# Carry, mean, variance, refinement steps and row maximum kept in spare columns of VectorE's own PSUM bank

## The reference, cut to what matters

```python
def _layernorm(x, axis=-1, eps=1e-05):
    m = jnp.mean(x, axis=axis, keepdims=True)
    v = jnp.var(x, axis=axis, keepdims=True)
    return (x - m) / jnp.sqrt(v + eps)

# attention, for each time step, batch row b and head h (16 heads of d = 16)
hebbian = jnp.einsum('bhi,bhj->bhij', v_t, k_t)
state = retention[None] * state + Gamma[None] * hebbian
y_t = jnp.einsum('bhij,bhj->bhi', W_static[None] + state, q_t)

# linear layer: each token is scaled by its own absolute maximum
amax = jnp.clip(jnp.max(jnp.abs(x), axis=-1, keepdims=True), EPS, None)
scale = amax / QMAX
x_q = jnp.clip(jnp.round(x / scale), -128, 127)

h = tok(x)                       # base + 0.1 * sum over domains of corrections
h = h + attn(_layernorm(h))
h = h + ffn(_layernorm(h))
```

## Time and profile before

| what | value |
|---|---|
| median of 3 runs | 365.59 us (363.73 to 366.17) |
| span of the profiled execution | 360.0 us |
| median above that span | 5.6 us |
| instructions | 4155 |
| DVE busy | 302.0 us (84%) |
| PE busy | 274.5 us (76%) |
| POOL busy | 207.5 us (58%) |
| ACT busy | 183.8 us (51%) |

### The profile page before, as it was taken

One profiled execution on the slowest core, in us unless ns is written; L12 is line 12 of the kernel. 1 busy time (PEld: TensorE's weight loads), 2 busy tenths in 40 slices (PEclk: granted clock), 3 DMA queues, 4 the chain that ended last, 5 costly groups with the idle time before them and its releaser, 6 DMA issues. The chain is left out here.

```text
span 360.0 us, 4155 instructions
## 1 busy us (share of the span) xinstructions
PE 274.5 (76%) x1214; PEld 141.5 (39%) x1214; DVE 302.0 (84%) x443; ACT 183.8 (51%) x336; POOL 207.5 (58%) x175
## 2 busy tenths in 40 slices
PE   5786899965979777965998498559978546747792
PEld 4674225531322353632333366223324213205581
DVE  0144098999999999999999999999999999999262
ACT  3236593455654704775768037576763168610152
POOL 5777676447873913747768317547876158970010
PEclk9899995996898799896999989887996956859899
DMA  6711200000010000000111000000210000001001
GB/s 168 251 46 49 75 7 2 3 0 0 13 50 26 0 3 1 0 0 29 36 50 33 4 1 0 0 31 0 74 44 3 0 0 0 0 15 46 0 2 58
DMA packets 10502, 10.07 MB, mean 28 GB/s; under 512 B 3344, under 2 KB 8944, under 8 KB 10480
## 3 DMA queue, kind: packets, MB, share of 16 engines
q1 hardware_dynamic: 9200, 7.70, 7.1%
q0 software_dynamic: 1280, 2.11, 2.1%
HBM read 4.95 MB, written 2.10 MB: 20 GB/s over the span
## 5 line engine op out<-in xcount | busy, mean ns | idle before, releaser
L380 POOL TENSOR_TENSOR uu<-vg,kk 128x512 f32<-128x512 f32 x128 | 160.1, 1275 | 99.7 <-ACT vg L566 93.7
L566 ACT ACTIVATE vg<-vr_ps,gam_sb 128x512 f32<-128x512 f32 x128 | 83.1, 687 | 20.3 <-PE vr_ps L882 12.6
L690 DVE TENSOR_TENSOR_SCAN zz<-r_ps,uu 128x512 f32<-128x512 f32 x64 | 77.2, 1214 | 10.3 <-POOL uu L380 10.3
L690 DVE TENSOR_TENSOR_SCAN zz<-r_ps,carry,uu 128x512 f32<-128x512 f32 x64 | 79.1, 1273 | 0.0
L711 DVE TENSOR_TENSOR zz<-zz,q_ps 128x1024 f32<-128x1024 f32 x64 | 76.4, 1196 | 0.0
L882 PE MATMUL vr_ps<-v_rows,selv 96*128 96x512 bf16 x100 | 40.5, 441 | 18.3 <-ACT vg L566 18.1
L896 PE MATMUL y_ps<-zz,sely 128*32 128x512 f32 x256 | 41.0, 717 | 15.2 <-DVE zz L711 15.2
L882 PEld LDWEIGHTS vr_ps<-v_rows,selv 96*128 96x128 bf16 x100 | 9.7, 102 | 55.8 <-ACT vg L566 38.9
L352 POOL TENSOR_TENSOR tok<-tok,bf 128x1024 f32<-128x1024 f32 x4 | 9.4, 2357 | 30.9 <-ACT tmp_b L482 29.3
L423 ACT ACTIVATE tok<-scr 128x512 f32<-128x512 f32 x16 | 9.5, 591 | 24.4 <-PE scr L812 17.5
L760 PE MATMUL scr<-wexp,emb_t 128*128 128x256 f32 x64 | 20.6, 479 | 1.0 <-ACT emb_t L415 1.0
(11 more groups left out here) (95 smaller groups left out, 413.3 us busy)
## 6 DMA issues: line engine op xcount, KB each, us to landing
v_rows<-v_part SPq DMA_DIRECT2D x84, 32.0 KB, 1.9
out_h<-tok SPq DMA_DIRECT2D x8, 256.0 KB, 2.2
wexp<-in_w_exp SPq DMA_DIRECT2D x1, 256.0 KB, 2.8
tok<-in_table,ids_sb POOLq DMA_INDIRECT x16, 2.8
wproj<-in_w_proj SPq DMA_DIRECT2D x1, 256.0 KB, 5.0
wv<-in_w_v SPq DMA_DIRECT2D x1, 256.0 KB, 4.8
wk<-in_w_k SPq DMA_DIRECT2D x1, 256.0 KB, 4.9
wq<-in_w_q SPq DMA_DIRECT2D x1, 256.0 KB, 5.3
```

What stands on the lines that cost most here:

```text
L380: pool.tensor_tensor(uu[:, slot % NU, :], vg[:, slot % NVG, :], kk[:, c % 2, hg, :], ALU.mult).then_inc(s_u, 1)
L566: act.activation(vg[:, slot % NVG, :], vr_ps[:, slot % NVR, :], ACT.Copy, scale=gam_sb[:, n:n + 1]).then_inc(s_vg, 1)
L690: dve.tensor_tensor_scan(zz[:, g % NZ, :], r_ps[:, n:n + 1].to_broadcast([P, T]), uu[:, g % NU, :], start, ALU.mult, ALU.add).then_inc(s_s ...
```

## The change

`carry`, `mv`, `am` and two of the three columns of `nr` lose their SBUF tiles and become views of `r_ps`: carry in columns 32 to 63, mean and variance in 64 to 79, the refinement's products in 80 to 95, the row maximum in 104 to 107. The reciprocal of the root stays in SBUF as `root`. The Newton step is written in another order: before, half the square of the root, times `ve`; now variance plus epsilon times the root, and that times minus one half times the root. So `ve` is read by ACT alone. The order of the instructions on every engine, their number and all semaphores are as before.

```diff
-        carry = sb("carry", [P, UNITS])
-        mv = sb("mv", [P, 2, TT, 2])
-        nr = sb("nr", [P, 2, 3, TT])
+        root = sb("root", [P, 2, TT])
-        am = sb("am", [P, TT])
...
         r_ps = ps("r_ps", [P, T])
+        carry = r_ps[:, UNITS:2 * UNITS]
+        mv = r_ps[:, 64:80].rearrange("p (n t s) -> p n t s", n=2, s=2)
+        nr = r_ps[:, 80:96].rearrange("p (n i t) -> p n i t", n=2, i=2)
+        am = r_ps[:, 104:108]
...
-                    r0, half_sq, fix = (nr[:, n, i, two] for i in range(3))
+                    r0, prod, fix = root[:, n, two], nr[:, n, 0, two], nr[:, n, 1, two]
                     link(dve.reciprocal(r0, sd[:, n, two]))
-                    link(dve.scalar_tensor_tensor(half_sq, r0, -0.5, r0, ALU.mult, ALU.mult))
-                    link(dve.tensor_tensor(fix, half_sq, ve[:, n, two], ALU.mult))
+                    link(dve.scalar_tensor_tensor(prod, mv[:, n, two, 1], LNEPS, r0, ALU.add, ALU.mult))
+                    link(dve.scalar_tensor_tensor(fix, prod, -0.5, r0, ALU.mult, ALU.mult))
                     link(dve.scalar_tensor_tensor(rstd[:, n, two], fix, 1.5, r0, ALU.add, ALU.mult))
```

## The result

The changed kernel takes 335.21 us (median, 334.41 to 339.93), the kernel before 364.71 us beside it (363.73 to 366.17). The ratio is 0.9185 with a 95% interval of 0.9138 to 0.9233: faster, by 29.5 us. The profiled execution has a span of 333.8 us and took 335.75 us; the span before was 360.0 us.

The account below looks back on a forecast made before the run. VectorE was taken to bound the kernel from first scan to last product. Gains of 9.7 + 12.8 + 7.3 = 29.8 us, less 1.3 and 0.5 off the path, gave 365.6 - 28.0 = 337.6, said as 338 us; range 334 to 352.

Parts of the forecast that it names:

- The bound and the cause: From first scan to last product VectorE is busy 283.64 of 289 us; its small all-SBUF operations wait for POOL.
- The terms of the gain: Waits removed on VectorE: carry copies 9.7 us, refinement steps 12.8, xs and ve 7.3, together 29.8 us.
- What is off the path: Of the 29.8 us, 1.3 near the first scans and masks and 0.5 at xs gain nothing, leaving 28.0.
- The stall at 54.28: A 0.73 us VectorE stall whose removal gains nothing, since VectorE idles 1.24 us before a mask at 62.06 anyway.
- What lies around the span: Median of timed runs 365.59 us, 5.6 above the profile's 360.0 us span; the change touches nothing outside the span.
- The price of PSUM operands: Scans and short VectorE operations newly using PSUM cost 0 extra; bounds 13.2 us dearer to 3.8 us cheaper.
- the nmr step: Two SBUF inputs yet a mean of 161 ns over 16, so the shared-port rule isn't the whole story.
- One-source operations that go on waiting: Rival: copies into PSUM and tensor_scalars out of it still wait for POOL; 17.0 us stay, 355 us; chance 0.08.
- Dearer PSUM: Rival: PSUM reads cost 59 ns each, giving 343 us on 88 short operations, 351 on all 224; chance 0.12.
- the slower case: Rival: each of 64 scans waits for the PSUM bank to drain; at 0.55 us each, 373 us; chance 0.03.
- Feeders: Rival: POOL, ScalarE and PE take back a third of the gain once a lead falls below zero; 347 us; chance 0.10.
- The change does nothing: Rival: the stall comes from small operations in a row, not from where operands lie; 366 us; chance 0.03.

Follow-up runs that it names:

- e5_poolwrite: The kernel before, with POOL's 128 products replaced by a memset of uu to a constant, so POOL writes without reading; one execution, 337.93 us.
- e4_reduce: The kernel before, carry still in SBUF but written by a tensor_reduce over one element instead of a tensor_copy; 357.83 us, ratio 0.9859.
- e8_onecol: The kernel before, with the carry copied by two tensor_copy instructions of one column each, SBUF to SBUF; 358.97 us, ratio 0.987.
- e6_order: The kernel before, with the refinement in the new order and all buffers in SBUF; 363.91 us, ratio 1.0012.
- e7_wlo_pool: The changed kernel, with the subtraction for the lowest part of the quantized weights moved from VectorE to POOL; 332.39 us, ratio 0.9151 to the kernel before.
- e3_am: The kernel before, with only the row maximum moved into the PSUM bank of r_ps; 358.35 us, ratio 0.9788.
- e1_carry: The kernel before, with only the carry tile moved into the PSUM bank of r_ps; 353.80 us, ratio 0.9735.
- e2_steps: The changed kernel, but with carry and the row maximum kept in SBUF as before; 345.39 us, ratio 0.9529 to the kernel before.
- the last three experiments: The changed kernel again, then with the weights' subtraction on POOL, then also with extra idle-time PE matmuls; 363.84, 361.92, 362.93 us, the kernel before 393.94.

## Why the prediction was right, by its steps

**The bound and the cause: right.** VectorE's busy time was the path, and its small operations waited for POOL. That they waited for POOL is shown by e5_poolwrite, where POOL's reading is gone and with it the wait of the steps, and by the ends: from the first scan on, every one over 0.25 us ends 0.01 to 0.03 us behind a POOL instruction. e4_reduce and e8_onecol (same data, same place, no wait) show that it takes a certain kind of access, and e6_order that the new order of the steps does nothing by itself.

**The terms of the gain: right.** Copies 32 x (442 - 149) = 9.4 us (predicted 9.7); steps 16 x (516 - 168 + 478 - 168 + 289 - 159) = 12.6 (12.8); xs and ve 8 x (902 - 160) + 16 x (260 - 159) = 7.6 (7.3). The sum is 29.6 for 29.8, and busy time fell by 29.2. The prediction didn't count the subtraction of e7_wlo_pool, which waits before and after.

**What is off the path: right in the stretch, wrong in the tail.** The stretch was to lose 28.0 less the tail's 1.5, 26.5 us; it lost 26.1. The stall at 54.28 was indeed taken back at 62 us, by a wait that grew by 0.74. The 1.5 us in the tail were gained too: from the first tok of the tail to the end there are 17.8 us where there were 19.3, and so it is in e3_am, where only the maximum moved. But from the last product to that tok there were 7.8 us where there had been 6.5, with PE's sum of y and first output matmuls at the lower level; at the higher one it is 4.9 (e7_wlo_pool, with 22.8 us of tail). So the tail as a whole lost only 0.2 us, and the span 26.2 for the predicted 28.0. The prediction had no term for PE's clock behind the last product, which differs between executions of one kernel.

**What lies around the span: the mis-sized term.** The prediction put 5.6 us around the span, the difference between the median and one profiled execution. The changed kernel's profiled execution took 335.75 us with a span of 333.8: 1.95 us around it. The other 3.6 us were the distance between a short execution and the median. Beside e5 to e8, 16 of 17 executions of the kernel before ranged over 360.95 to 364.93 us. The median therefore fell by more (29.5) than the two profiled spans did (26.2), and the forecast of 338 was 2.8 us too high. That 28.0 lies between the two is in part luck, since PE's clock in the tail alone moves a profiled span by up to 3 us. It may also be why a usual execution of the kernel before is longer than the profiled one; that wasn't settled.

**The price of PSUM operands: right, close to zero.** Scans that take their start value from PSUM stay at 1273 ns in the mean of the 64, those without one at 1214 (VectorE's timeline of the changed kernel: a scan without a carry, then one that starts from it):

```profile
108.10 1.21 DVE L691 TENSOR_TENSOR_SCAN zz<-r_ps,uu 128x512 f32<-128x512 f32 x1
...
110.34 1.28 DVE L691 TENSOR_TENSOR_SCAN zz<-r_ps,uu 128x512 f32<-128x512 f32 x1
```

Writing PSUM costs 7 to 9 ns more (the copy 149 against the 140 of a free one, steps 168 against 161), reading it 10 less for the two tensor_scalar operations (ve 159 against 169) and 2 less for nmr and rstd. The Trainium skill's 62 extra cycles for PSUM as the source ("VectorE: DVE Perf Modes", section "The TRN2 errata — SBUF-src ops pay a fixed extra latency per instruction") don't show in this case: ve, xs and nmr read PSUM at 159 to 160 ns.

**A reading that was wrong.** The prediction took the nmr step, two SBUF inputs and 161 ns, as a sign that the rule on shared ports isn't the whole story. It was a matter of when: nmr stands behind three steps that wait for POOL's running product, and in none of its 16 executions was a product running when it began. Before the change, nmr starts at 87.10 us, behind the rstd step that ends at 87.07, and the six products of the earlier trace rows end at 87.05. With that, the rule of the Trainium skill ("SBUF — State Buffer", section "Who interferes with whom") agrees with what was measured, down to the two sorts of wait in e5_poolwrite: two SBUF inputs contend with POOL's reading alone, two-port modes with its writing too. What it doesn't tell is why xs waited there for several memsets in a row (last section).

**The rivals.** One-source operations that go on waiting: refuted, copy and xs are short. Dearer PSUM, and the slower case with it: refuted. Feeders: POOL's narrowest lead after 62 us fell from 1.2 to 0.8 us, and never to zero. The change does nothing: refuted. A rival that the prediction didn't have, that the stall shifts to the next operation, may be true in part when only some of the operations are freed: 2.7 of 5.9 us in e3_am and 2.1 of 10 in e4_reduce, but 0.2 of 9.4 in e1_carry, and in e2_steps the rest waited 1.3 less. When all are freed, nothing is left to take it over but the subtraction, which grew by 0.13 us.

## What to carry to other kernels

When a group of tiny VectorE operations has a mean far above its shortest, lay its longest ones beside GpSimd's timeline: if they end where GpSimd's instructions end, they wait for them, and the wait is recorded as their own time. What freed them here was a PSUM operand: the source of a tensor_scalar, the destination of a copy, one of the two inputs of a step, at no more than 9 ns each. A copy was also freed by being written as a reduce, or as two copies of one element. Free all of them, since otherwise those that are left may wait longer. Don't take one profiled span and a median of other executions as two ends of the same run.

## What wasn't expected of the hardware

A copy of two elements waits for GpSimd and a copy of one doesn't (means of 442 ns against 126 and 140, same data). xs waited for three memsets of GpSimd in a row in e5_poolwrite, not just for the one that was running: it began at 142.41 and ended at 143.57, and they ran from 142.09 to 143.54. First VectorE's timeline of that kernel:

```profile
142.41 1.16 DVE L639 TENSOR_SCALAR xs<-am 128x2 f32<-128x2 f32 x1
```

Then POOL's:

```profile
142.09 1.45 POOL L380 MEMSET uu<- 128x512 f32 x3
```

The wait goes both ways: the POOL product that ran beside the subtraction took 1.72 us before and 1.73 after the change, while no other took over 1.30, and in e7_wlo_pool, where the subtraction isn't on VectorE, none does.

And beside the last three experiments every kernel was some 29 us longer, from a standstill in the head that the profile doesn't explain, with the scan stretch unchanged.
